# A mixture-of-experts and state-space layer: fixed last tiles, eight early dense groups, and the state's input product taken in the router's pass

## The chip, the cores and the metric

The kernel runs on one core of a Trainium2 chip. The metric is the device time of one execution in microseconds (us). The kernel before took 1827.65 us, the median of three runs (1825.58 to 1830.5). One further execution was profiled; all rows below are from it.

## The reference

The input x has 16 x 512 = 8192 tokens (rows) of 256 features. Everything is float32.

```
xn  = layernorm(x)                          # no weights
out = x + dense(xn) + moe(xn)

dense(x):                                   # a state-space block and a gated feed-forward
  u  = rmsnorm(x) * ssm_w
  Bu = u @ B_w.T                            # 64 states per row
  h_b = sigmoid(log_lambda) * h_(b-1) + Bu_b   # lax.scan over swapaxes(Bu, 0, 1)
  x  = x + h @ C_w.T + D_skip * u
  z  = rmsnorm(x) * ffn_w
  return x + (silu(z @ w1.T) * (z @ w3.T)) @ w2.T      # 688 hidden

moe(h):                                     # 32 experts, 8 chosen per row, inner size 128
  scores  = sigmoid(h @ gate_w.T);  sc = scores + gate_bias
  keep the 4 best of 8 expert groups (by the sum of their two best sc), then the 8 best experts
  weights = 2.5 * scores of the chosen / their sum
  routed  = sum over the chosen of weight * (silu(h @ w_gate.T) * (h @ w_up.T)) @ w_down.T
  shared  = (silu(h @ sh_gate.T) * (h @ sh_up.T)) @ sh_down.T      # 256 hidden
  return routed + shared
```

## The kernel before

The 8192 rows are 64 tiles of 128; four tiles make one of 16 dense groups, and 32 tiles one half of the expert work. Each engine has its instruction stream written out by hand, and semaphores tie them. In order of time:

1. The router's pass (`a0_...`). For each group VectorE and ScalarE normalise x into `rows_of` (half 0 in `big`, half 1 in `xe`), TensorE transposes (`a0_transpose`), ScalarE copies to `a0_xT`, TensorE multiplies with the router's weights (`a0_router`), ScalarE copies the product (L598) and, when it is transposed back, the logits. SP loads x and the constants.
2. SP stores two blocks of zero rows, 9216 KB each, over the last 64 tiles of `sorted_rows` of either half (L398). They pad what no row fills.
3. Nine early dense groups (`FIRST = 9`). The steps s = 0 to 7 of a group are eight hidden tiles: shared expert first (s < 2), then the feed-forward. Woven into them is the preparation of the next group: `transpose_x`, `bu_product` (L1232), VectorE's `bu_scale` (L948), `bu_transpose` (L1239), `scan` (L954), `y_product` (L1245), `make_x1`, `make_z`, `transpose_z`. Also woven in is the routing (`route`, `route_late`): for each half VectorE picks the experts, ranks the rows with TensorE's help, works out the base of each expert's tiles (`r_bases`), and the slot of each row in `sorted_rows` (`r_slot_table`); `r_weights` ends it and signals `routing_done`.
4. GpSimd's scatter. One indirect DMA (L546) per tile and choice writes 128 rows of xn with their weights to their slots, 256 per half. Ahead of it 16 padding stores of GpSimd and 16 of SP (32 of SP for half 1) zero what is left of each expert's last tile.
5. The expert pairs. A half has 288 tiles of 128 sorted rows, worked off in 144 pairs. `one_expert(n)` is true for the first `SAME` = 128 pairs of a half: both tiles belong to one expert, and its gate and up weights are copied once and used for 256 columns. In the other 16 pairs each tile has its own expert, with two weight copies (L1100) and twice the matmuls of half the width (L1348). All expert weights stand in `big`, on top of what the routing and half 0 had there, so their last pieces are loaded when half 0 has been scattered (L420). The results go to DRAM; GpSimd gathers them per row (L557) and VectorE adds them up (`sum_step`), half 0 during the pairs of half 1.
6. Seven late dense groups, the first of which is prepared after the last pair. The adding up of half 1 (`combine`) is woven into them.

Of the kernel before, what the change touches and what calls it, by code (L numbers as in the profile page):

```python
# [5 lines left out]
P = 128  # L6
# [6 lines left out]
ds = bass.ds  # L13
# [6 lines left out]
E = 32  # L20
# [29 lines left out]
def build(nc, x, log_lambda, BT, CT, D_skip, ssm_w, ssm_w_col, ffn_w_col, w13T, w2T, gateT, gate_bias, wexp,  # L50
# [13 lines left out]
    SAME = HT * K // 2  # L64
    USED = 2 * SAME - E
    SPAN = NSLOT + E * P
# [6 lines left out]
    FIRST = 9  # L73
    LATE = range(FIRST, GROUPS)
    QUARTER = HT // 4
# [5 lines left out]
    parts = nc.dram_tensor("parts", [T, D], F32).ap()  # L81
    te_dram = nc.dram_tensor("te_dram", [HALVES, 2, P * TE_C], U32).ap()

    with ExitStack() as ctx:
# [40 lines left out]
        bT = sb("bT", [P, DC, N_STATE])  # L125
        cT = sb("cT", [N_STATE, D])
        gT = sb("gT", [P, DC, E])
# [41 lines left out]
        ne, ntf, endt, base, nt_f, ones_e, full_f, full, unused_f, unused_i = (scratch(E) for _ in range(10))  # L169

        two_f, two, odd, end_odd, apart, cut, first_odd, te_odd, te_late = (logits[:, k * E:(k + 1) * E] for k in range(9))
        two_u = two_f.bitcast(U32)
        first_odd, te_odd, te_late = first_odd[:, 0:1], te_odd[:, 0:TE_C], te_late[:, 0:TE_C]
        nt_u, full_u, unused_u = nt_f.bitcast(U32), full_f.bitcast(U32), unused_i.bitcast(U32)
        in_part = nt_f
# [6 lines left out]
        pad_starts = [scratch(E).bitcast(U32) for _ in range(HALVES)]  # L182
# [12 lines left out]
        ARENA = 9472  # L195
# [9 lines left out]
        bu = take(GT * N_STATE).rearrange("p (t n) -> p t n", n=N_STATE)  # L205
# [12 lines left out]
        a0_lT = [take(G)[0:E, :] for _ in range(2)]  # L218
# [30 lines left out]
        a0_lT_ready = sem("a0_lT_ready")  # L249
# [11 lines left out]
        starts_ready = sem("starts_ready")  # L261
        padded = sems("padded", HALVES)
        padded_by_pool = sem("padded_by_pool")
# [8 lines left out]
        bu_ready = sem("bu_ready")  # L272
        bu_scaled = sem("bu_scaled")
        buT_ready = sem("buT_ready")
# [15 lines left out]
        scattered = [sems(f"scattered{h_}_", 4) for h_ in range(HALVES)]  # L290
# [13 lines left out]
        gathered = sems("gathered", DEEP)  # L304
        part_loaded = sems("part_loaded", RING)
# [5 lines left out]
        CONSTS = 16  # L311
        WEXP_LOADS = 1 + 1 + 4
# [9 lines left out]
        def xn_of(g):  # L322

            if g in LATE:
                return xn_late
            return rows_of[g // 8][:, g % 8 * GT:(g % 8 + 1) * GT, 0:D]
# [32 lines left out]
        def scattered_all(eng, half):  # L359

            for j in range(4):
                eng.wait_ge(scattered[half][j], 16 * K * QUARTER)
# [3 lines left out]
        def _(sp):  # L366
# [9 lines left out]

            for n in range(GROUPS):
                load_x_a0(n)
            for dst, src in ((bT[:, :, :], BT), (ssmw_col[:, :], ssm_w_col),
                             (skip_w[:, :], D_skip.partition_broadcast(P)),  # L380
# [12 lines left out]
            for n in range(GROUPS, GROUPS + 4):  # L393
                load_x_a0(n)

# [5 lines left out]

            def store_padding(half, es):
                sp.wait_ge(starts_ready, half + 1)
                sp.wait_ge(padded[half], 16)
                for e in es:
                    start = sp.value_load(pad_starts[half][0:1, e:e + 1], min_val=0, max_val=SPAN - P)
                    sp.dma_start(sorted_rows[half][ds(start, P), :], pad_row).then_inc(padded[half], 16)
# [18 lines left out]
            store_padding(0, range(E // 2))  # L426
            for g in range(FIRST - 1):
                if g + 4 < FIRST:
# [5 lines left out]
                if g == 3:  # L434
                    store_padding(1, range(E))
                if g == 4:
                    turn_tile_experts(1)
                if g == 5:
                    sp.wait_ge(routing_done, 2)
                    sp.wait_ge(padded[0], 16 * (E // 2 + 1))  # L440
                    sp.wait_ge(padded_by_pool, 16 * (E // 2))
                    sp.wait_ge(padded[1], 16 * (E + 1))
                    load_wexp(0, AT_X)
            sp.wait_ge(x_used, FIRST)
            load_wexp(AT_X, AT_ROWS)
            sp.wait_ge(xposed, FIRST)
            for j in range(4):
                sp.wait_ge(scattered[0][j], 16 * K * QUARTER)
                load_wexp(AT_ROWS + j * QUARTER * ROW, AT_ROWS + (j + 1) * QUARTER * ROW)
            store_part(FIRST - 1)  # L450


# [13 lines left out]
            sp.wait_ge(zposed, FIRST)  # L466
            sp.wait_ge(gu_ready, CH * (FIRST - 1) + 2)
            sp.wait_ge(rms_z_ready, FIRST)
            for n in range(RING):
                load_rows(n)  # L470
            for par in range(2):
                sp.wait_ge(part_stored[par], 16 * len(range(par, FIRST, 2)))
            for m in range(ALL + 2):
                if m < ALL:
# [4 lines left out]
                    if m + RING < ALL:  # L479
                        load_rows(m + RING)  # L480
                n = m - 2
# [11 lines left out]
            sp.wait_ge(wgu_ready, ALL)  # L493
            for g in range(FIRST, FIRST + 4):
                load_x(g, g)
            for i in range(HT, HT + GT):
                load_part(i)
            for g in LATE:
                for t in range(GT):
                    store_out((g - 1) * GT + t)  # L500
                    if t == 2 and g + 4 < GROUPS:
                        sp.wait_ge(x_used, g + 1)
                        load_x(g + 4, g + 4)
# [7 lines left out]
        def _(pool):  # L511
# [16 lines left out]
            nc.gpsimd.iota(unused_u, pattern=[[1, E]], base=NTILE, channel_multiplier=0)  # L528
# [904 lines left out]
```

## Time and profile before

| | |
|---|---|
| median of three runs | 1827.65 us |
| profiled execution | 1828.46 us, span of its records 1826.8 us |
| TensorE | 1732.0 us busy (95%), granted clock 0.969 on average |
| VectorE | 986.1 us (54%) |
| ScalarE | 653.4 us (36%) |
| GpSimd | 1042.6 us (57%) |
| DMA | 383.71 MB, 210 GB/s on average |
| chain that ended last | TensorE 89%, VectorE 7%, others 4% |

The span runs from the first to the last instruction; the time of the execution is 1.66 us longer. The chain is the sequence of work that ended last, followed back from the end. Expert products (L1348) are 29% of it, the dense gate and up products (L1263) 19%. A share of busy time is a mean over stages: which wait ends last has to be read at the borders between them. TensorE's granted clock has two levels, 2.4 GHz (1.00) and 1.2 GHz (0.50).

### The profile page before, as it was taken

What the parts mean: (1) busy time and instruction counts of PE and PEld (TensorE: products, weight loads), DVE (VectorE), ACT (ScalarE), POOL (GpSimd) and SP (SyncE); (2) the same over time, 40 slices, a digit from 0 to 9 for tenths busy, and PEclk for the clock granted to TensorE, in tenths of its full rate; (3) what the DMA queues carried; (4) which work ended last, traced back from release to release, by engine and by line L of the source; (5) the groups of instructions that cost most, each with busy time, mean ns of one, the idle gap of its engine ahead of it and who ended that gap; (6) DMA issues with size and microseconds to landing.
All of it is one profiled execution on the core that took longest, in us unless ns stands there. A gap on an engine that the chain in (4) does not pass through costs nothing.

```text
span 1826.8 us, 26818 instructions
## 1 busy us (share of the span) xinstructions
PE 1732.0 (95%) x7846; PEld 1259.9 (69%) x7848; DVE 986.1 (54%) x2832; ACT 653.4 (36%) x1349; POOL 1042.6 (57%) x1058
## 2 busy tenths in 40 slices
PE   7797899899998999999999999999999969999996
PEld 3464565566666888888889888888888846666663
DVE  7487646633313444444445566666666535555555
ACT  6520221222213444444444444444444422222220
POOL 0002777777777777773000566666656077777773
PEclk9798999899998999999999999999999969999998
DMA  5964333636378999997555899999899554443332
GB/s 171 323 224 139 134 140 115 223 128 252 126 277 274 297 292 300 293 296 248 180 176 179 255 295 274 287 276 288 275 284 277 175 158 123 123 121 110 110 110 75
DMA packets 270790, 383.71 MB, mean 210 GB/s; under 512 B 30916, under 2 KB 235832, under 8 KB 269880
## 3 DMA queue, kind: packets, MB, share of 16 engines
q1 hardware_dynamic: 220584, 236.94, 41.1%
q0 software_dynamic: 49920, 145.03, 24.1%
q8 instruction: 66, 1.08, 0.2%
q14 instruction: 76, 0.62, 0.1%
q10 hardware_dynamic: 144, 0.03, 0.0%
HBM read 189.47 MB, written 192.42 MB: 209 GB/s over the span
## 4 chain that ended last, share of the span: by engine, by line
PE 89%; DVE 7%; issue 1%; ACT 1%; DMA 1%; DVEq 0%; SPq 0%; ACTq 0%
PE ps L1348 29%; PE ps L1263 19%; PE ps L1362 14%; PE ps L1280 11%; PE ps L1336 7%; PE ps L1183 2%; PE ps L1245 2%; PE ps L1216 2%; PE ps L1255 1%; PE ps L1232 1%; PE ps L1176 1%; DVE big L1009 1%; DMA big<-in_x 0%; PE ps L1239 0%; DVE arena L991 0%
## 5 line engine op out<-in xcount | busy, mean ns | idle before, releaser
L557 POOL DMA_INDIRECT xe<-results,slots x384 | 391.9, 1020 | 395.8 <-DMA results<-arena 217.4
L1348 PE MATMUL ps<-arena 128*128 128x256 f32 (+1 forms) x2560 | 573.5, 369 | 1.5 <-ACT arena L675 1.5
L1348 PEld LDWEIGHTS ps<-arena 128*128 128x128 f32 x2560 | 428.6, 190 | 106.1 <-ACT arena L675 66.0
L1100 DVE COPY arena<-big 128x512 f32 x320 | 138.7, 442 | 345.4 <-PE ps L1348 318.6
L546 POOL DMA_INDIRECT sorted_rows<-big,slots x256 | 260.5, 1017 | 84.0 <-issue 77.8
L1362 PE MATMUL ps<-big,arena 128*128 x1152 | 296.4, 380 | 0.3 <-DVE arena L1108 0.3
L546 POOL DMA_INDIRECT sorted_rows<-xe,slots x256 | 248.3, 970 | 78.1 <-issue 78.1
L1263 PE MATMUL ps<-arena,w 128*128 128x512 f32 x640 | 288.4, 593 | 0.0
L648 ACT ACTIVATE arena<-ps 128x512 f32<-128x512 f32 (+1 forms) x128 | 76.4, 597 | 559.4 <-PE ps L1263 515.5
L991 DVE TENSOR_TENSOR arena<-arena,ps 128x512 f32<-128x512 f32 (+1 forms) x128 | 88.0, 688 | 329.3 <-ACT arena L648 328.2
L680 ACT ACTIVATE arena<-ps 128x256 f32<-128x256 f32 x288 | 110.6, 384 | 377.0 <-PE ps L1348 377.0
L1362 PEld LDWEIGHTS ps<-big,arena 128*128 128x128 f32 x1152 | 196.4, 190 | 15.4 <-issue 0.7
L1263 PEld LDWEIGHTS ps<-arena,w 128*128 128x128 f32 x640 | 122.2, 191 | 119.5 <-issue 115.2
L1280 PE MATMUL ps<-w,arena 128*128 128x256 f32 (+1 forms) x768 | 186.3, 385 | 1.7 <-DVE arena L991 1.7
L675 ACT ACTIVATE arena<-ps 128x512 f32<-128x512 f32 x288 | 172.1, 597 | 26.1 <-PE ps L1336 11.0
L1336 PE MATMUL ps<-ident,arena 128*128 128x128 f32 x1152 | 173.8, 274 | 6.4 <-DMA arena<-sorted_rows 6.4
L1280 PEld LDWEIGHTS ps<-w,arena 128*128 128x128 f32 (+1 forms) x768 | 142.8, 191 | 50.7 <-issue 31.1
L1117 DVE TENSOR_SCALAR arena<-ps,wcol 128x256 f32<-128x256 f32 x288 | 139.0, 483 | 68.1 <-PE ps L1362 60.4
L690 ACT ACTIVATE arena<-ps,wcol 128x256 f32<-128x256 f32 x288 | 136.6, 474 | 92.6 <-PE ps L1362 91.0
L1336 PEld LDWEIGHTS ps<-ident,arena 128*128 128x128 f32 x1152 | 143.5, 141 | 32.8 <-issue 6.9
L557 POOL DMA_INDIRECT big<-results,slots x128 | 130.4, 1019 | 39.0 <-issue 39.0
L1263 PE MATMUL ps<-arena,shgu 128*128 128x512 f32 x256 | 123.4, 638 | 7.1 <-DVEq L819 7.1
(186 smaller groups left out, 1402.8 us busy)
## 6 DMA issues: line engine op xcount, KB each, us to landing
arena<-sorted_rows SPq DMA_DIRECT2D x288, 288.0 KB
results<-arena SPq DMA_DIRECT2D x288, 256.0 KB, 3.6
sorted_rows<-big SPq DMA_DIRECT2D x2, 9216.0 KB, 47.3
big<-in_x SPq DMA_DIRECT2D x32, 512.0 KB, 4.5
sorted_rows<-big SPq DMA_DIRECT2D x48, 144.0 KB, 1.9
xe<-results,slots POOLq DMA_INDIRECT x384, 4.0
out<-xe SPq DMA_DIRECT2D x48, 128.0 KB, 3.9
big<-in_wexp SPq DMA_DIRECT2D x1, 5632.0 KB, 19.3
```

Of the source, the lines that this page charges most:

```text
L546: pool.indirect_dma_start(out=sorted_rows[half], out_offset=bass.IndirectOffsetOnAxis(ap=slots[:, half * HT + t, k:k + 1], axis=0), in_=ro ...
L557: pool.indirect_dma_start(out=gathered_at[place(i)][:, k, :], out_offset=None, in_=results[half], in_offset=bass.IndirectOffsetOnAxis(ap=s ...
L675: nc.scalar.activation(rT[n % 2], ps[:, n % 2, :], ACT.Copy).then_inc(rT_ready, 1)
L680: nc.scalar.activation(eg[n % 2], ps[:, 2 + n % 2, 0:2 * P].rearrange("p (s i) -> p s i", s=2), ACT.Silu).then_inc(eg_ready, 1)
L690: nc.scalar.activation(ey[n % RING][:, 0, :], ps[:, 4 + 2 * (n % 2), 0:D], ACT.Copy, scale=wcol[:, n % RING, 0:1]).then_inc(ey_act, 1)
L1100: last = nc.vector.tensor_copy(wgu[n % 2][:, s, :], big[:, ds(at_w, 4 * INNER)])
L1117: tsc(ey[n % RING][:, 1, :], ps[:, 5 + 2 * (n % 2), 0:D], wcol[:, n % RING, 1:2], None, ALU.mult).then_inc(ey_dve, 1)
L1263: last = mm(ps[:, 2 + 2 * (s % 2) + u, :], w[:, u, c, lo:lo + P], src[:, c, :], start=c == 0, stop=c == DC - 1)
L1280: last = mm(ps[:, 6 + t // 2, (t % 2) * D:(t % 2 + 1) * D], h[c % HR][at_p, t * P:(t + 1) * P], w, start=False, stop=s == CH - 1 and t % 2 ...
L1336: last = tp(ps[:, n % 2, j * P:(j + 1) * P], rows[n % RING][:, s, c * P:(c + 1) * P], ident[:, :])
L1348: last = mm(ps[:, 2 + n % 2, (2 * u + s) * P:(2 * u + end) * P], wgu[n % 2][:, s, at_w:at_w + INNER], rT[n % 2][:, (2 * c + s) * P:(2 * c ...
L1362: last = mm(ps[:, 4 + 2 * (n % 2) + s, 0:D], eh[n % 2][:, s, :], big[:, ds(at_w + 2 * D, D)], start=True, stop=True)
```

## The change

- **Fixed last tiles.** Each expert's last, partly filled tile now has a fixed place: tile 256 + e for expert e, inside the region that is zeroed at the start. The padding stores that depended on the counts go (16 on GpSimd, 48 on SP). Only full tiles are paired, so a half has 96 pairs of one expert and 48 of two. The slot table has a second correction, and the tile-to-expert table four more small steps.
- **Eight early groups.** `FIRST` is 8. Group 8 is prepared inside group 7, and its `xT`, `zT` and part are stored to DRAM and read back behind the expert pairs; its eight steps are the first of the late stage.
- **The input product in the router's pass.** `first_w` holds the state's and the router's weights side by side, one product gives 64 + 32 rows. ScalarE copies them and issues a store of the 64 rows to `bu_dram`. The reciprocal norms are turned to rows (`turn_rinv`, `copy_rinv`) and stored too. SP reads both back for each group (`load_bu`); VectorE multiplies and scans. `bu_product`, `bu_scale` and `bu_transpose` are gone, the scan stands at s = 2 rather than 3, the y product at s = 3 rather than 4.
- The scatter signals in eighths of a half rather than quarters.

```diff
-    SAME = HT * K // 2
-    USED = 2 * SAME - E
-    SPAN = NSLOT + E * P
+    FULL_TILES = HT * K
+    SAME = FULL_TILES // 2 - E
+    USED = FULL_TILES - E
+    SPAN = NSLOT
-    FIRST = 9
+    FIRST = HT // GT
...
@@ SP @@
+            def load_bu(n):
+                sp.wait_ge(bu_stored[n % 2], 16 * (n // 2 + 1))
+                sp.wait_ge(rinv_stored, 16 * (n // 8 + 1))
+                if n:
+                    sp.wait_ge(y_ready, n)
+                sp.dma_start(bu, bu_dram[n]).then_inc(bu_loaded, 16)
+                sp.dma_start(hs, rinv_dram[n * GT:(n + 1) * GT, :].rearrange("t p -> (t p)").partition_broadcast(N_STATE)
+                             ).then_inc(bu_loaded, 16)
...
             for n in range(GROUPS, GROUPS + 4):
                 load_x_a0(n)
+            load_bu(0)
...
-            store_padding(0, range(E // 2))
+            load_bu(1)
             for g in range(FIRST - 1):
...
                 store_part(g)
+                load_bu(g + 2)
...
@@ GpSimd @@
-            pool.wait_ge(starts_ready, 1)
-            pool.wait_ge(padded[0], 16)
-            for e in range(E // 2, E):
-                start = pool.value_load(pad_starts[0][0:1, e:e + 1], min_val=0, max_val=SPAN - P)
-                pool.dma_start(sorted_rows[0][ds(start, P), :], pad_row).then_inc(padded_by_pool, 16)
...
@@ ScalarE @@
                 act.wait_ge(a0_products_ready, g + 1)
-                nc.scalar.activation(a0_lT[g % 2], ps[0:E, 4 + g % 2, :], ACT.Copy).then_inc(a0_lT_ready, 1)
+                if g >= 2:
+                    act.wait_ge(bu_stored[g % 2], 16 * (g // 2))
+                nc.scalar.activation(a0_first[g % 2], ps[0:N_STATE + E, 4 + g % 2, :], ACT.Copy
+                                     ).then_inc(a0_first_ready, 1)
+                act.wait_ge(a0_first_ready, g + 1)
+                act.dma_start(bu_dram[g], a0_first[g % 2][0:N_STATE, :]).then_inc(bu_stored[g % 2], 16)
...
@@ VectorE @@
             def scan(n):
-                dve.wait_ge(buT_ready, n + 1)
-                nc.vector.tensor_tensor_scan(hs, lam_b[:, :], ps[0:N_STATE, 1, :], 0.0, ALU.mult, ALU.add
-                                             ).then_inc(hs_ready, 1)
+                dve.wait_ge(bu_loaded, 32 * (n + 1))
+                do(tt(bu, bu, hs, ALU.mult))
+                nc.vector.tensor_tensor_scan(hs, lam_b[:, :], bu, 0.0, ALU.mult, ALU.add).then_inc(hs_ready, 1)
...
                     if more and s == 2:
-                        bu_scale(g + 1)
-                    if more and s == 3:
                         scan(g + 1)
...
-            dve.wait_ge(ey_act, ALL)
-            a1_norm(FIRST)
-            bu_scale(FIRST)
-            scan(FIRST)
-            make_x1(FIRST)
-            make_z(FIRST)
...
@@ TensorE @@
-                    if more and s == 2:
-                        bu_product(g + 1)
-                    if more and s == 3:
-                        bu_transpose(g + 1)
-                    if more and s == 4:
+                    if more and s == 3:
+                        pe.wait_ge(xT_ready, g + 2)
                         y_product(g + 1)
...
-            transpose_x(FIRST)
-            bu_product(FIRST)
-            bu_transpose(FIRST)
-            y_product(FIRST)
-            transpose_z(FIRST)
+            pe.wait_ge(xT_reloaded, 16)
```

ScalarE in the router's pass, before; L598 is the copy of the product, L602 that of the logits:

```order
L572 ACTIVATE rstd<-mv,ln_eps 128x4 [waits var_ready]
L598 ACTIVATE arena<-ps 32x512 [waits a0_products_ready]
L602 ACTIVATE big<-ps 128x128 [waits a0_logits_ready]
L580 ACTIVATE big<-big,nmr,rstd 128x256 [waits nmr_ready]
L580 ACTIVATE big<-big,nmr,rstd 128x256
```

The same place now:

```order
L602 ACTIVATE rstd<-mv,ln_eps 128x4 [waits var_ready]
L630 ACTIVATE arena<-ps 96x512 [waits bu_stored0,a0_products_ready]
L633 DMA bu_dram<-arena 64x512 [waits a0_first_ready]
L651 ACTIVATE big<-ps 128x128 [waits a0_logits_ready]
L610 ACTIVATE big<-big,nmr,rstd 128x256 [waits nmr_ready]
L610 ACTIVATE big<-big,nmr,rstd 128x256
```

Between the two copies stands the issue of a store, behind a wait for the copy ahead of it.

SP's queue at the end of the router's pass, before; the two rows of 128x64x288 are the zero blocks:

```order
L392 DMA shd<-in_shdT 128x512
L369 DMA big<-in_x 128x4x256 [waits a0_xn_act,a0_xn_dve] x4
L398 DMA sorted_rows<-big 128x64x288 [waits routing_consts_made]
L398 DMA sorted_rows<-big 128x64x288
L406 TENSOR_LOAD big [waits padded0,starts_ready]
```

And now, with the input product and the factors of groups 0 and 1 (`bu_dram`, `rinv_dram`):

```order
L416 DMA shd<-in_shdT 128x512
L385 DMA big<-in_x 128x4x256 [waits a0_xn_act,a0_xn_dve] x4
L398 DMA arena<-bu_dram 64x512 [waits rinv_stored,bu_stored0]
L399 DMA arena<-rinv_dram 64x512
L423 DMA sorted_rows<-big 128x64x288 [waits routing_consts_made]
L423 DMA sorted_rows<-big 128x64x288
L398 DMA arena<-bu_dram 64x512 [waits y_ready,rinv_stored,bu_stored1]
L399 DMA arena<-rinv_dram 64x512
L385 DMA big<-in_x 128x4x256 [waits x_used]
```

Group 0's loads stand ahead of the zero blocks, group 1's behind them.

SP's queue where the experts begin, now; before, the row loads (`arena<-sorted_rows`) waited for the dense groups alone, and the last piece of expert weights stood ahead of them:

```order
L438 DMA big<-in_wexp 128x4096 [waits x_used]
L486 DMA parts<-arena 128x4x256
L461 DMA arena<-sorted_rows 128x2x288 [waits scattered0_3,scattered0_2,scattered0_4,scattered0_1,scattered0_5,scattered0_0,scattered0_6,z_ready,scattered0_7,y_ready,xT_stored]
L461 DMA arena<-sorted_rows 128x2x288 x3
L438 DMA big<-in_wexp 128x1152 [waits scattered0_7]
L495 DMA kept_zT<-arena 128x1024 [waits zT_ready]
L442 DMA parts<-arena 128x4x256 [waits part_ready]
```

Rows, the last weights, the kept `zT` and group 7's part now follow the last scatter.

## Rows read from the trace of the kernel before

**Rows 1.** Chain of waits: start us, us, what; starts of three groups.
```profile
461.65 7.06 PE ps L1263 x16
508.13 7.06 PE ps L1263 x16
...
1770.21 7.06 PE ps L1263 x16
```

**Rows 2.** Timeline, SP and TensorE, before the experts: start us, us, instruction, idle before.
```profile
549.92 0.38 SPq L424 DMA_DIRECT2D parts<-arena  x1
...
556.72 3.78 PE L1348 MATMUL ps<-arena 128*128 128x256 f32 x8 [0.77 <-ACT arena L675]
```

**Rows 3.** The scatter's line: duration ns min/median/max, first and last start.
```profile
L546 POOL DMA_INDIRECT sorted_rows<-big,slots x256: 957/963/4916, 181.2 to 518.5; - x128
L546 POOL DMA_INDIRECT sorted_rows<-xe,slots x256: 959/963/1187, 519.7 to 844.8; - x128
...
DMA to landing us min/median/max: 2.4/2.5/16.5
```

**Rows 4.** Timeline of VectorE in groups 0 and 1.
```profile
110.39 0.42 DVE L948 TENSOR_TENSOR arena<-ps,rinv 128x256 f32<-128x256 f32 x1
...
113.50 1.20 DVE L954 TENSOR_TENSOR_SCAN arena<-lam_b,ps 64x512 f32<-64x512 f32 x1
117.33 0.69 DVE L991 TENSOR_TENSOR arena<-arena,ps 128x512 f32<-128x512 f32 x1 [2.63 <-ACT arena L648]
...
153.26 1.22 DVE L857 TENSOR_TENSOR big<-big 128x1024 f32<-128x1024 f32 x1
...
166.86 1.23 DVE L875 TENSOR_TENSOR big<-big 128x1024 f32<-128x1024 f32 x1
```

**Rows 5.** The zero blocks' line: issue ns min/median/max, starts, landing.
```profile
L398 SPq DMA_DIRECT2D sorted_rows<-big x2: 1458/13469/25480, 61.6 to 63.1; - x2
...
DMA to landing us min/median/max: 33.7/47.3/60.9
```

**Rows 6.** Timeline of ScalarE in the router's pass, one group of 16.
```profile
50.98 0.59 ACT L598 ACTIVATE arena<-ps 32x512 f32<-32x512 f32 x1 [0.35 <-PE ps L1183]
51.47 0.25 ACT L602 ACTIVATE big<-ps 128x128 f32<-128x128 f32 x1
```

**Rows 7.** Timeline: the issues of two small loads.
```profile
0.94 0.43 ACTq L566 DMA_DIRECT2D gT<-in_gateT  x1
...
49.95 1.09 SPq L392 DMA_DIRECT2D cT<-in_CT  x1
```

**Rows 8.** Timeline of TensorE, prologue and group 0; the last row from the chain.
```profile
75.47 3.78 PE L1245 MATMUL ps<-cT,arena 64*128 64x256 f32 x8 [1.37 <-DVE arena L954]
...
102.82 1.90 PE L1232 MATMUL ps<-bT,arena 128*128 128x64 f32 x16
104.55 1.95 PE L1280 MATMUL ps<-shd,arena 128*128 128x256 f32 x8
...
116.59 1.99 PE L1245 MATMUL ps<-cT,arena 64*128 64x256 f32 x8
...
176.17 0.44 PE ps L1239 x4
```

**Rows 9.** Chain at pair 128 of half 1; and busy times of the stretch behind it.
```profile
1404.97 1.82 PE ps L1348 x8
...
1408.09 1.87 PE ps L1348 x16
...
1408.09:1458.90 50.81, 50.55 (x382) 45.98 (x382) 31.94 (x103) 23.05 (x48) 6.49 (x7) 1.00 0.62 190
```

**Rows 10.** Timeline behind the pairs: last output, first product of group 9.
```profile
1459.95 0.48 DVE L1117 TENSOR_SCALAR arena<-ps,wcol 128x256 f32<-128x256 f32 x1 [0.91 <-PE ps L1362]
...
1489.32 9.10 PE L1263 MATMUL ps<-arena,shgu 128*128 128x512 f32 x16
```

**Rows 11.** Timeline of GpSimd: its last gather.
```profile
1801.96 0.95 POOL L557 DMA_INDIRECT big<-results,slots  x1 [0.30 <-issue]
```

More of the change, by code:

```diff
@@ L217, in build @@
         a0_xT = [take(DC * G).rearrange("p (c n) -> p c n", c=DC) for _ in range(2)]
-        a0_lT = [take(G)[0:E, :] for _ in range(2)]
+        a0_first = [take(G)[0:N_STATE + E, :] for _ in range(2)]
+        rinvT = take(P)[0:HT, :]
         at[0] = 0
@@ L288, in build @@
         part_stored = sems("part_stored", 2)
[L290 removed]
+        scattered = [sems(f"scattered{h_}_", PIECES) for h_ in range(HALVES)]
         wexp_loaded = sem("wexp_loaded")
@@ L359, in scattered_all @@
         def scattered_all(eng, half):
-            for j in range(4):
-                eng.wait_ge(scattered[half][j], 16 * K * QUARTER)
+            for j in range(PIECES):
+                eng.wait_ge(scattered[half][j], 16 * K * PIECE)
         @block.sync
@@ L756, in _ @@
                     a0_stats(g + 4)
+                if g == -3:
+                    dve.wait_ge(router_loaded, 16 * FIRSTS)
+                    for c in range(DC):
+                        last = tsc(first_w[:, c, 0:N_STATE], first_w[:, c, 0:N_STATE], ssmw_col[:, c:c + 1], None,
+                                   ALU.mult)
+                    last.then_inc(bT_folded, 1)
+                if g == 5:
+                    rms_x(0)
+                if g == 6:
+                    invert_rms_x(0)
+            rms_x(1)
+            invert_rms_x(1)
             def r_pairs(half):
@@ L849, in r_bases @@
                 tsc(base, base, float(P), 1.0, ALU.mult, ALU.add)
-                tsc(apart, apart, float(P), None, ALU.mult)
-                do(tt(full, full, unused_f, ALU.add))
-                tsc(pad_starts[half], full, float(P), None, ALU.mult).then_inc(starts_ready, 1)
+                tsc(apart_part, apart_part, float(P), None, ALU.mult)
+                do(tsc(apart, apart, float(P), None, ALU.mult))
             def r_slot_table(half):
-                by_expert, past = (a.rearrange("p (e t) -> p e t", t=HT) for a in (work, wt))
@@ L857, in r_slot_table @@
-                do(tt(past, by_expert, cut.unsqueeze(2).to_broadcast([P, E, HT]), ALU.is_ge))
-                do(tt(past, past, apart.unsqueeze(2).to_broadcast([P, E, HT]), ALU.mult))
+                by_expert, past, past_full = (a.rearrange("p (e t) -> p e t", t=HT) for a in (work, wt, table))
+                tt(past, by_expert, cut.unsqueeze(2).to_broadcast([P, E, HT]), ALU.is_ge)
+                do(tt(past_full, by_expert, cut_part.unsqueeze(2).to_broadcast([P, E, HT]), ALU.is_ge))
+                tt(past, past, apart.unsqueeze(2).to_broadcast([P, E, HT]), ALU.mult)
@@ L859, in r_slot_table @@
+                do(tt(past_full, past_full, apart_part.unsqueeze(2).to_broadcast([P, E, HT]), ALU.mult))
+                do(tt(wt, wt, table, ALU.add))
                 do(tt(work, work, wt, ALU.add))
```

286 lines of the change are left out of this document (162 added, 124 removed).

## The prediction

> **What bounds the kernel now.** I read the chain of waits first, then the stage borders on it. TensorE carries the chain in three stages: nine early dense groups, 288 expert pairs, seven late dense groups. Dense groups follow each other 46.5 us apart (461.65 to 508.13, [rows 1]). The ninth ends where its part is stored, at 549.92, and the first expert product starts at 556.72 [rows 2]. GpSimd's scatter of half 0 was over by then: 256 indirect DMAs from 181.2 to 519.7, 338.5 us or 1.32 us each, landing 2.5 us after issue [rows 3]. So today the experts wait for the ninth group, and the scatter has about 30 us to spare. VectorE's routing for half 0 comes before the scatter; it ends at 166.86 + 1.23 = 168.1 [rows 4].
>
> The change removes the ninth group from the early stage, so the scatter becomes the candidate for the bound. Everything ahead of it (router pass, padding, routing) then counts in full, which it did not before.
>
> **Router pass.** ScalarE gets a store of the input product for every group, behind a wait for its own copy. The copy takes 0.59 us and its successor starts after 0.49 [rows 6]; the wait adds 0.10, its semaphore some 0.05 (estimate), and the issue 0.43 by ScalarE's only issue before [rows 7]. Of these 0.58 us the idle 0.35 ahead of the same copy [rows 6] hides a part. I take 0.27 for what is left, 13 times until the loads of x are done: 3.5 us. The bounds are 0 and, with SP's dearest small issue of 1.09 us for 64 partitions [rows 7], (0.15 + 1.09 - 0.35) x 13 = 11.6 us. Turning the reciprocals to rows twice makes ScalarE wait for TensorE and VectorE; I put 2 us (bounds 0 and 4). The router's product grows from 32 to 96 output rows with the same 512 columns, hidden. SP issues two more loads ahead of the padding, 0.9. The padding starts 6.4 us later.
>
> **The wait that is added.** The two padding stores are issued at 61.6 and 63.1, and land 33.7 and 60.9 us later, at 95.3 and 124.0 [rows 5]. The second lands 28.7 us after the first though it was issued 1.5 us behind it: SP's queue works them off one after the other. The load of the input product for group 1 now stands on that queue behind both. With the 6.4 us the padding is through at 130.4 and the load, 256 KB with its factors, at about 132.2. VectorE waits for it at step s=2 of group 0, in order, with the top-8 steps, h tiles and the whole routing chain behind it; by its steps before (the input product's scaling at 110.39, [rows 4]) it would be there near 115. Multiplication and scan (1.2 us, [rows 4]) end at T = 134.1. Without the change the scan ended at 113.50 + 1.20 = 114.7.
>
> From the scan to the end of routing took 168.1 - 114.7 = 53.4 us. Now the y product comes before gate/up product 4. TensorE will have stood still for over 15 us, and after such a stop rows show the lower clock: the y product took 3.78 us in the prologue and 1.99 in group 0 [rows 8]. So until h tile 4: y 3.8, the down product 3.1 (partly slow), gate/up 3.5 (half of 7.06, [rows 1]), gate and semaphores 0.9, together 11.3 (7.9 at the full clock), where it had been 117.33 - 114.7 = 2.6 [rows 4]. That adds 8.7. The slot table gets three more operations of 1.22 us [rows 4] and the base computation loses about 1.5 us of small ones: +2.2. Routing ends at T + 64.3 = 198.4.
>
> The Trainium skill, "DMA: Bandwidth & Descriptors", section "Queues, rings and completion order", says that each DMA engine consumes one queue's descriptors in ring order but takes turns between the queues of SP and ACT. By that rule the load on SP's queue must wait while ScalarE's stores need not; the trace agrees for SP's queue [rows 5], and no run here shows the turns.
>
> **Scatter and the experts' start.** The small padding stores, 16 by GpSimd and 16 + 32 by SP, go; the scatter starts 0.3 us after the routing rather than 13 us after it. At 1.32 us each, less 3 us for the vanished stores, 256 take 335 us (bounds 324 at the steady 1.27 of the second half's 325.1 us [rows 3], and 345). 198.7 + 335 = 533.7, landed 536.2. Then SP issues four row loads, the last expert piece, the kept z and the last part, 2.8 MB. Before it was 1.7 MB in 556.72 - 549.92 = 6.8 us [rows 2]; the extra 1.1 MB at some 330 GB/s (9.4 MB per 28.7 us, [rows 5]) and two issues more give 11.2. First expert product at 547.4, 9.3 us earlier.
>
> Would the dense groups end later? Each loses the input product, 104.55 - 102.82 = 1.73, and its transposes, 0.44, 2.2 us together [rows 8]. From the end of routing to the ninth group's start it was 508.13 - 168.1 = 340.0 [rows 1, 4]; now it is 340.0 - 6 x 2.2 + 2.2 (the second slot table) = 329.0, so the eighth ends at 527.4, and with some 8 us of seam experts could start at 535.6. No: the scatter is last, and the early groups' saving pays nothing.
>
> **Experts.** Pairs with one expert fall from 256 to 192, those with two rise from 32 to 96. A one-expert pair takes 1408.09 - 1404.97 = 3.12 us, one with two 3.18, as its product part is 1.87 against 1.82 [rows 9]; 64 x 0.056 = +3.6 us. The second weight copy on VectorE is hidden: in the stretch of two-expert pairs with sums it was busy 31.94 of 50.81 us. Last pair's output ends at 1459.95 + 0.48 = 1460.4 [rows 10], 903.7 after the first; now X = 547.4 + 903.7 + 3.6 = 1454.7.
>
> **Late stage.** Before, the prologue of group 9 stood open: 1460.4 to 1489.32, 28.9 us [rows 10]. Now xT is reloaded inside the pairs, zT needed only at s=2, and group 8 starts 0.6 us after X. The load and normalisation of x for group 9 come just late: 1.5 us. So 0.6 + 45.8 + 6 x 44.3, and from the last group's start to the end 1826.8 - 1770.21 = 56.6 as before [rows 1]: 368.9 us, where it was 366.4. GpSimd's last gather began at 1801.96 [rows 11], 342 after the pairs' end; it has one group more, so it stays hidden.
>
> **Sum.** 1454.7 + 368.9 = 1823.6 against the span 1826.8, -3.2. The profiled execution took 1828.46, 1.7 more than its span; so 1825.2, and 1824.4 against the median of 1827.65. In short: -9.3 at the first border, +3.6 in the pairs, +2.5 after them.
>
> **Rivals.**
> *No queueing.* If the load of group 1 passes the padding, VectorE scans at once, T is 116.6, the clock stays up, routing ends 60.9 later at 177.5, the scatter has landed at 515.3, first product at 526.5: 1804. Against it: the 28.7 us between the two landings. For it: only that the load is small.
> *Quicker scatter.* At 324 us the scatter lands at 525 and the dense end (535.6) decides: 1813. For it the second half's 325 us; against, that half ran beside less VectorE work.
> *ScalarE held by SP's issue.* The second padding issue kept SP 25.5 us [rows 5]. If ScalarE's last stores cannot be issued meanwhile, it stands until about 95, group 0 starts near 115 instead of 93, reaches its scan at 137, T = 139.2, with TensorE at its full clock: routing ends at 139.2 + 60.9 = 200.1, 1826. The Trainium skill, "Perfetto Trace Analysis", section "DMA Instruction — HWDGE (DVE, Sync)", says that the block that writes descriptors is shared between sequencers, which would be this mechanism; no row here shows it.
> *Slower.* ScalarE's 16 stores. Each us they add to the router pass moves padding, scan, routing, scatter and experts alike, since nothing later has slack. At 1.09 us per issue the pass grows by 11.6 rather than 3.5, and with the turning at its bound of 4 that is 1834.5. From 0.72 us per issue on the change gains nothing. For it the SP row of 1.09; against it ScalarE's own 0.43.
>
> **How the numbers follow.** What can be told from no change is about 0.3%, 5.5 us: faster is below 1822.2, slower above 1833.1. The forecast has 0.47, own range 1815 to 1833 (faster 0.13, same 0.27, slower 0.07). No queueing 0.15 (faster), quicker scatter 0.12 (faster), ScalarE held 0.10 (same 0.07, slower 0.03), slower stores 0.16 (slower 0.14, same 0.02). Sum: faster 0.40, same 0.36, slower 0.24. The range 1806 to 1838 leaves out most of the first rival and the far end of the last.
>
> **What would show it.** VectorE idle at its multiply in group 0 until the padding has landed, near 132; L546's counterpart starting near 199; TensorE idle some 15 to 20 us between the eighth group and the first expert product, released by rows or the last piece of expert weights; late groups 44.3 us apart; no gap of 29 us behind the pairs. The prediction is wrong if the scan of group 1 ends before 120, if the scatter ends before TensorE's early groups, if the router pass lengthens by more than 10 us, or if a two-expert pair takes over 3.25 us.

## The result and the profile after

The changed kernel took 1840.08 us, the median of five runs (1835.92 to 1840.98), beside 1827.81 for the kernel before on the same chip: a ratio of 1.0059, 95% interval 1.0047 to 1.0071. It is slower by 12.3 us. The forecast was 1824.4, in a range of 1806 to 1838. The profiled execution has a span of 1838.3 us, 14.7 more than the 1823.6 of the prediction's sum.

**The wait on SP's queue.** The timeline of SP after the router's pass:

```profile
67.25 0.59 SPq L399 DMA_DIRECT2D arena<-rinv_dram  x1
67.89 27.24 SPq L423 DMA_DIRECT2D sorted_rows<-big  x2
95.24 29.63 SPq L398 DMA_DIRECT2D arena<-bu_dram  x1
124.91 1.40 SPq L399 DMA_DIRECT2D arena<-rinv_dram  x1
```

L423 is the padding (L398 in [rows 5]), L398 and L399 are the two loads of the input product and its factors. Behind the padding not only the transfer waits: the issue of a 128 KB load stands on SP for 29.63 us. The padding's own line, and ScalarE's stores of the input product, first the issue in ns with the first and last start, then the landing:

```profile
L423 SPq DMA_DIRECT2D sorted_rows<-big x2: 578/13598/26617, 67.9 to 68.5; - x2
...
DMA to landing us min/median/max: 33.7/48.4/63.1
```

```profile
L633 ACTq DMA_DIRECT2D bu_dram<-arena x16: 452/453/516, 19.5 to 71.7; - x16
...
DMA to landing us min/median/max: 2.3/3.3/6.4
```

Padding started 6.3 us later than in [rows 5], at 67.9; the forecast was 68.0. ScalarE's 16 stores took 0.45 us each. Two were issued after 68.3, while SP stood in the second padding issue, and neither they nor ScalarE were held. VectorE and TensorE at the scan of group 1 (in square brackets the idle time before the instruction and what ended it):

```profile
133.18 0.68 DVE L1025 TENSOR_TENSOR arena<-arena 64x512 f32<-64x512 f32 x1 [17.07 <-DMA arena<-rinv_dram]
133.89 1.22 DVE L1026 TENSOR_TENSOR_SCAN arena<-lam_b,arena 64x512 f32<-64x512 f32 x1
```

```profile
135.25 3.75 PE L1305 MATMUL ps<-cT,arena 64*128 64x256 f32 x8 [21.48 <-DVE arena L1026]
138.93 3.78 PE L1340 MATMUL ps<-w,arena 128*128 128x256 f32 x8
142.51 4.58 PE L1323 MATMUL ps<-arena,w 128*128 128x512 f32 x8
```

From 135.2 to 147.1 TensorE's granted clock was 0.61 on average, the lower level for the first two of these rows. At the full clock the same three took 1.99 us [rows 8], 1.89 (from 146.92) and 3.60 (from 148.65): the clock cost 4.6 us behind the stop.

**Routing and scatter.** Routing of half 0 ended at 199.59 + 1.23 = 200.8, where it was 168.1 [rows 4]. The scatter, half 0 and half 1, to be set beside [rows 3]:

```profile
L574 POOL DMA_INDIRECT sorted_rows<-big,slots x256: 956/960/4566, 201.8 to 544.0; - x128
```

```profile
L574 POOL DMA_INDIRECT sorted_rows<-xe,slots x256: 956/960/1212, 545.3 to 870.5; - x128
```

Half 0 takes 342.2 us from first to last start, 337.3 before; half 1 takes 325.2 and 325.1.

**The border to the experts.** TensorE's eighth group starts at 499.96 and is followed by VectorE's last add to its part; then SP, TensorE, ScalarE and VectorE:

```profile
499.96 1.55 PE L1323 MATMUL ps<-arena,shgu 128*128 128x512 f32 x3
...
550.28 1.09 PE L1394 MATMUL ps<-ident,arena 128*128 128x128 f32 x4 [6.00 <-DMA arena<-sorted_rows]
562.73 2.90 PE L1406 MATMUL ps<-arena 128*128 128x256 f32 x6 [11.36 <-DVE arena L1166]
```

```profile
546.81 1.98 SPq L461 DMA_DIRECT2D arena<-sorted_rows  x4
548.84 0.47 SPq L438 DMA_DIRECT2D big<-in_wexp  x1
549.35 0.43 SPq L495 DMA_DIRECT2D kept_zT<-arena  x1
549.83 0.44 SPq L442 DMA_DIRECT2D parts<-arena  x1
```

```profile
561.10 0.60 ACT L732 ACTIVATE arena<-ps 128x512 f32<-128x512 f32 x1 [17.62 <-DMA parts<-arena]
```

```profile
544.32 1.28 DVE L1069 TENSOR_TENSOR arena<-arena,ps 128x512 f32<-128x512 f32 x2 [3.21 <-PE ps L1340]
562.16 0.77 DVE L1166 COPY arena<-big 128x512 f32 x2 [16.55 <-issue]
```

The scatter is last at 546.8, but the dense groups end at 545.6, level with it. Then SP's 2.8 MB are moved until 561, and the first product (L1406, L1348 before) starts at 562.73, 6.0 us later than in [rows 2]. TensorE's waits in groups 1 and 3, for VectorE:

```profile
201.78 1.65 PE L1340 MATMUL ps<-shd,arena 128*128 128x256 f32 x3 [11.37 <-DVE arena L1062]
...
317.29 0.88 PE L1305 MATMUL ps<-cT,arena 64*128 64x256 f32 x3 [3.94 <-DVE arena L1026]
```

The first is 7.06 us in the kernel before (at 169.05), and the second, a wait for the scan, is not there. Group 4 has one like the first, 10.80 us for 6.56.

**Pairs and late groups.** The expert line, first and last start, and the first gate and up products behind the pairs and in the last group:

```profile
L1406 PE MATMUL ps<-arena x3072: 275/371/766, 562.7 to 1467.0; 128*128 128x256 f32 x96, 128*128 128x128 f32 x96
L1420 PE MATMUL ps<-big,arena x1152: 379/379/478, 570.3 to 1469.1; 128*128 x192
```

```profile
1470.35 1.96 PE L1323 MATMUL ps<-arena,shgu 128*128 128x512 f32 x4 [0.83 <-DVE arena L1185]
...
1781.60 4.99 PE L1323 MATMUL ps<-arena,shgu 128*128 128x512 f32 x11
```

The gap of 29 us behind the pairs [rows 10] is gone, and behind the first of them late groups follow each other 44.3 us apart (1516.09 to 1781.60 in six steps) instead of 46.5.

### The profile page after: what moved, and what is told of

Same layout as the page of the kernel before. It is cut to its first block, busy times and chain, and to the rows that moved or that the text cites. A ratio compares the mean times of both kernels' runs of the same rounds, so it can differ in the third digit from the quotient of the medians.

```text
span 1838.3 us, 27059 instructions
## 1 busy us (share of the span) xinstructions
PE 1702.5 (93%) x8040; PEld 1250.5 (68%) x8042; DVE 1010.7 (55%) x2899; ACT 654.9 (36%) x1352; POOL 1042.3 (57%) x1042
## 4 chain that ended last, share of the span: by engine, by line
PE 69%; POOL 14%; issue 5%; DVE 4%; SPq 3%; DMA 2%; ACT 2%; ACTq 0%; DVEq 0%; POOLq 0%
PE ps L1406 29%; POOL sorted_rows L574 14%; PE ps L1420 14%; PE ps L1323 10%; PE ps L1394 7%; PE ps L1340 6%; SPq L398 2%; SPq L423 1%; PE ps L1305 1%; PE ps L1315 1%; PE ps L1290 1%; DMA bu_dram<-arena 1%; DMA parts<-arena 1%; DMA big<-in_x 1%; ACT arena L622 1%
## 5 line engine op out<-in xcount | busy, mean ns | idle before, releaser
L1406 PE MATMUL ps<-arena 128*128 128x256 f32 (+1 forms) x3072 | 577.1, 336 | 12.0 <-DVE arena L1166 11.4
L1406 PEld LDWEIGHTS ps<-arena 128*128 128x128 f32 x3072 | 455.7, 191 | 106.7 <-ACT arena L732 76.6
L574 POOL DMA_INDIRECT sorted_rows<-big,slots x256 | 265.5, 1037 | 276.3 <-DVEq L947 198.6
L1166 DVE COPY arena<-big 128x512 f32 x384 | 160.0, 438 | 356.1 <-PE ps L1406 322.1
L702 ACT ACTIVATE arena<-ps 128x512 f32<-128x512 f32 (+1 forms) x128 | 76.3, 596 | 565.8 <-PE ps L1323 524.4
L1340 PE MATMUL ps<-w,arena 128*128 128x256 f32 (+1 forms) x768 | 191.7, 394 | 3.4 <-DVE arena L1062 3.4
L1340 PEld LDWEIGHTS ps<-w,arena 128*128 128x128 f32 (+1 forms) x768 | 147.1, 195 | 61.0 <-issue 37.6
## 6 DMA issues: line engine op xcount, KB each, us to landing
big<-in_wexp SPq DMA_DIRECT2D x1, 5632.0 KB, 18.7
```

Source lines behind the costliest of these rows:

```text
L574: pool.indirect_dma_start(out=sorted_rows[half], out_offset=bass.IndirectOffsetOnAxis(ap=slots[:, half * HT + t, k:k + 1], axis=0), in_=ro ...
L1166: last = nc.vector.tensor_copy(wgu[n % 2][:, s, :], big[:, ds(at_w, 4 * INNER)])
L1340: last = mm(ps[:, 6 + t // 2, (t % 2) * D:(t % 2 + 1) * D], h[c % HR][at_p, t * P:(t + 1) * P], w, start=False, stop=s == CH - 1 and t % 2 ...
L1406: last = mm(ps[:, 2 + n % 2, (2 * u + s) * P:(2 * u + end) * P], wgu[n % 2][:, s, at_w:at_w + INNER], rT[n % 2][:, (2 * c + s) * P:(2 * c ...
```

## The experiments

Eleven kernels. Ratios are to the kernel before, with 95% intervals; runs 7 and 8 were executed once.

| run | edit | us | ratio |
|---|---|---|---|
| changed kernel | | 1840.1 | 1.0059 (1.0047 to 1.0071) |
| 1 | padding behind the load of group 1 | 1821.1 | 0.9965 (0.9952 to 0.9979) |
| 2 | only half 1's padding behind it | 1821.0 | 0.9969 (0.9957 to 0.9981) |
| 3 | padding left, load issued by ScalarE | 1822.2 | 0.9976 (0.9966 to 0.9987) |
| 4 | looser waits at the border | 1836.9 | 1.0058 (1.0044 to 1.0071) |
| 5 | kernel before + fixed tiles alone | 1840.7 | 1.0074 (1.0060 to 1.0088) |
| 6 | 1 + 4 + order of the border's transfers | 1815.9 | 0.9933 (0.9920 to 0.9947) |
| 7, 8 | 6 + repeated adds | 1820.6, 1827.0 | |
| 9 | 6 + scan from PSUM | 1818.2 | 0.9952 (0.9939 to 0.9966) |
| 10 | 6 without the fixed tiles | 1815.5 | 0.9937 (0.9924 to 0.9951) |
| 11 | 10 + scan from PSUM | 1818.0 | 0.9949 (0.9935 to 0.9963) |

### Run 1: the padding behind the load

```
-            for half in range(HALVES):
-                sp.dma_start(sorted_rows[half][USED * P:NSLOT, :] ...).then_inc(padded[half], 16)
...
             load_bu(1)
+            for half in range(HALVES):
+                store_padding(half)          # the same store
```

> Both padding stores are issued by SP behind the load of the input product for group 1 instead of ahead of it. Theory (queue order is the loss): the load lands before VectorE needs it at 116.1, the idle of 17.07 us before its multiply and TensorE's 21.5 us go, routing ends near 181 instead of 200.8, scatter 181.5 to 525, dense end near 524, first expert product near 543: 20 us less than 1840.1, about 1820. Rival (the DMA engines are simply full, the order does not matter): the load still lands near 133 and the time stays at 1840. Second rival (scatter and dense end do not follow the routing one to one, for the padding now runs beside group 0): under half of the 20 us comes back, about 1832.

Measured 1821.05, 19.0 less. SP's timeline, and the scatter's line:

```profile
84.20 0.45 SPq L398 DMA_DIRECT2D arena<-bu_dram  x1
84.70 0.59 SPq L399 DMA_DIRECT2D arena<-rinv_dram  x1
85.33 24.88 SPq L423 DMA_DIRECT2D sorted_rows<-big  x2
110.25 29.06 SPq L385 DMA_DIRECT2D big<-in_x  x1
```

```profile
L576 POOL DMA_INDIRECT sorted_rows<-big,slots x256: 956/960/4573, 183.1 to 525.0; - x128
```

The wait of 29 us has not gone; it now stands before a load of x that nobody wants before group 3. Scan ends at 116.9 (135.1), scatter starts at 183.1 (201.8), the first weight copy at 542.2 (562.2): 18.3, 18.7, 20.0 us. What the scan loses, the end loses. By the ratios the gain is 17 us rather than 19. TensorE stood for 4.4 us instead of 21.5, and its clock was at the lower level behind it all the same:

```profile
117.00 3.75 PE L1307 MATMUL ps<-cT,arena 64*128 64x256 f32 x8 [4.41 <-DVE arena L1028]
```

### Run 2: one store ahead, one behind

```
+            store_padding(0)
             load_bu(1)
+            store_padding(1)
```

> Only the padding store of half 1 is issued behind the load of the input product for group 1; that of half 0 stays ahead of it. Theory (the load waits exactly for what stands ahead of it on SP's queue): half 0's store is through at 101.6, the load lands at 104 to 110, still before VectorE's 116.1, so the whole stall goes as with both moved: about 1820. If the stall grows with the time of the store rather than ending at its landing, or if the store of half 1 takes engine time from the load, half of it stays (idle of 5 to 10 us before the multiply): about 1830.

1820.97, and no wait before the multiply. SP:

```profile
67.80 0.58 SPq L423 DMA_DIRECT2D sorted_rows<-big  x1
84.17 10.76 SPq L398 DMA_DIRECT2D arena<-bu_dram  x1
94.97 1.37 SPq L399 DMA_DIRECT2D arena<-rinv_dram  x1
```

The load's issue stands for 10.8 us, until 94.9, behind one store of 9.4 MB, and for 29.6 behind two. One store ahead fits into the time until VectorE wants the load at 116; two do not.

### Run 3: the load on ScalarE's queue

```
-            load_bu(1)                       # SP
...
+            act.wait_ge(y_ready, 1)
+            act.dma_start(bu, bu_dram[1]).then_inc(bu_loaded, 16)
+            act.dma_start(hs, rinv_dram[GT:2 * GT, :] ...).then_inc(bu_loaded, 16)
             zT_copy(0)
```

> The padding stays where it is; the load of the input product for group 1 and its factors is issued by ScalarE, ahead of its zT copy of group 0. Theory (the queue, not the DMA engines, holds the load): issued near 85 to 93, landed 3 to 10 us later in the middle of the padding, no stall at VectorE, two issues of 0.5 us each ahead of group 0: about 1821. Rival (16 DMA engines busy with 9.4 MB per half hold any load): landed only after 131, time 1840 or more, since ScalarE's issue may stand as well.

1822.24. ScalarE's timeline and what the view of DMAs says of its queue (KB each, us from issue to landing), in the middle of the padding:

```profile
89.81 0.47 ACTq L724 DMA_DIRECT2D arena<-bu_dram  x1
90.31 1.35 ACTq L725 DMA_DIRECT2D arena<-rinv_dram  x1
```

```profile
arena<-bu_dram ACTq DMA_DIRECT2D x1, 128.0 KB, 5.7
arena<-rinv_dram ACTq DMA_DIRECT2D x1, 128.0 KB, 6.7
```

So the DMA engines were not closed to the load; the queue was. Both loads landed by 97.0, with the padding in flight until about 133. The Trainium skill, "DMA: Bandwidth & Descriptors", section "Queues, rings and completion order", says that a DMA engine takes turns between the queues of SP and ACT; this run agrees. The Trainium skill, "Perfetto Trace Analysis", section "DMA Instruction — HWDGE (DVE, Sync)", says that the block that writes descriptors is shared between sequencers; no holding of ScalarE's issues is seen here, 0.47 and 1.35 us while SP stood in the padding's two issues for 27.5.

### Run 4: looser waits at the border

```
# ScalarE: both part_stored waits dropped; SP: dropped
# VectorE:
-            for par in range(2):
-                dve.wait_ge(part_stored[par], 16 * len(range(par, FIRST, 2)))
+            dve.wait_ge(part_stored[0], 16 * len(range(0, FIRST, 2)))
+            dve.wait_ge(part_kept, 16)
```

> Behind the eighth dense group VectorE waits for the stored parts of even groups and the kept part only (the others are not overwritten by expert tiles), ScalarE's first copy of turned rows for none, SP for none. Padding as in the changed kernel. Theory (the last part's store, fourth in the queue, costs the seam about 5 us): first weight copy near 557 instead of 562.16, bounded by the last piece of expert weights, issued at 548.84; 5 us less, about 1835. Rival (all the transfers of the seam share one bandwidth and land together, 2.8 MB): within 1 us of 1840.

```profile
557.54 0.78 DVE L1162 COPY arena<-big 128x512 f32 x2 [14.06 <-issue]
```

The first weight copy came at 557.5, as expected. The median fell by 3.2 us, but the ratio is that of the changed kernel (1.0058 and 1.0059), so a gain in the whole time is not shown by this run. Between the scatter's landing and this copy there are now 10.6 us, most of them for the last piece of expert weights, issued at 549.0.

### Run 5: the fixed tiles alone

The edit is the diff of the tiles put on the kernel before: `SAME` 96, `USED`, `r_bases`, `r_slot_table`, `r_tile_experts`, and no small padding stores; nine early groups, no store or load of the input product.

> The kernel before with the fixed zeroed last tiles alone: nine early dense groups, the input product per group, no store or load of it. By the theory (the early dense groups end last in this form, so a scatter that starts sooner gains nothing, and the pairs cost 64 x 0.056 us more): scatter starts near 171 instead of 181.2 and ends near 512, the ninth group's part is stored near 550 as before, pairs +3.6, and 2 us of slot table on VectorE's way: 1831 to 1833 against 1827.7. Rival (the tiles carry a gain of their own, since 48 small stores and their waits are gone): 1824 or less.

1840.74: 12.9 us more, not 4, and the profiled execution shows 9.9 of them. TensorE at the ninth group and the first pair, and the expert and scatter lines:

```profile
513.77 1.55 PE L1243 MATMUL ps<-arena,shgu 128*128 128x512 f32 x3
```

```profile
561.88 1.65 PE L1328 MATMUL ps<-arena 128*128 128x256 f32 x3 [0.77 <-ACT arena L655]
```

```profile
L1342 PE MATMUL ps<-big,arena x1152: 379/379/478, 571.4 to 1470.2; 128*128 x192
```

```profile
L526 POOL DMA_INDIRECT sorted_rows<-big,slots x256: 956/960/4962, 171.0 to 507.7; - x128
```

The ninth group starts 5.6 us later than in [rows 1]: 3 us from the slot table of half 0, 3 from that of half 1, on VectorE, for which TensorE waits in groups 1 and 4. From first product to last down product the pairs take 908.3 instead of 902.8, +5.5. The scatter, 10 us earlier and without the small stores, takes 336.7 between its starts instead of 337.3: taking the stores away made it no shorter. Both expectations fell; this part alone costs as much as the whole change.

### Run 6: padding and border together

```
+            sp.dma_start(kept_zT, zT...).then_inc(zT_stored, 16)
+            store_part(FIRST - 1)
             scattered_all(sp, 0)
-            for n in range(RING):
-                load_rows(n)
+            load_rows(0)
             load_wexp_over_rows(PIECES - 1)
+            for n in range(1, RING):
+                load_rows(n)
```

> Both repairs: the padding is issued behind the load for group 1, and at the seam the kept z and the last part are stored before the wait for the scatter, then row load 0, the last piece of expert weights, row loads 1 to 3, with the looser waits of the fourth kernel. Theory (seam bounded by what is issued between the scatter's landing and the first weight copy): scatter landed near 527.5, row load and piece issued in 1 us and 0.87 MB landed 4 us later, first weight copy near 533 instead of 542.2: 9 us less than 1821.0, 1812. Rival (dense groups end level with the scatter, so stores move behind the last group and nothing but the 4.7 us of the loosened wait is won): 1816.

```profile
524.84 0.33 SPq L493 DMA_DIRECT2D kept_zT<-arena  x1
526.96 0.37 SPq L442 DMA_DIRECT2D parts<-arena  x1
529.32 0.37 SPq L463 DMA_DIRECT2D arena<-sorted_rows  x1
529.74 0.49 SPq L438 DMA_DIRECT2D big<-in_wexp  x1
```

```profile
536.25 0.76 DVE L1165 COPY arena<-big 128x512 f32 x2 [9.38 <-issue]
```

1815.91, the fastest with run 10, and 0.67% below the kernel before. The copy came 6.0 us earlier than in run 1, 9 had been expected: the scatter's last landing slipped from 527.5 to 529.3 beside the two stores that were moved ahead of it, and the piece of weights took 5.2 us rather than 4. Of the 15 us between scatter and first copy, 7 are left.

### Runs 7 and 8: does VectorE hold the scatter?

```
# 7, groups 2 to 7, three times ahead of the add itself:
+                        do(tt(part_of(n), x_of(n), x1, ALU.add))       # both inputs from SBUF
# 8, likewise:
+                        ... tt(x1[...], z[...], ps[:, b, :] ..., ALU.add)  # one from PSUM
```

> As the kernel with padding and seam, and for the groups 2 to 7 VectorE's add of x and x1 (both read from SBUF, 1.22 us) is done four times instead of once, to the same place: 18 more operations, 22 us of VectorE. Theory (GpSimd's indirect DMA is held while VectorE runs an operation that reads both inputs from SBUF): the 256 scatters, 265.1 us of busy time at a floor of 0.96 each, grow by 0.7 to 3.5 us per group, 4 to 21 in all. Rival (the long scatters are chance, or of the DMA engines): busy time within 2 us of 265.

> The same with the two adds into x1 (one input from SBUF, one from PSUM, 1.28 us the pair) done four times: as much more time of VectorE as in the run with repeated adds of x and x1. Theory: only two inputs from SBUF hold GpSimd, so the 256 scatters stay within 2 us of 265. Rival (any work of VectorE slows GpSimd): they grow as in that run. In both runs the early groups may end later, by up to 3.8 us a group.

The scatter's group, of run 7 and of run 8 (busy us, mean ns, idle):

```profile
L575 POOL DMA_INDIRECT sorted_rows<-big,slots x256 | 263.8, 1030 | 258.4 <-DVEq L946 180.7 <-issue 77.7
```

```profile
L575 POOL DMA_INDIRECT sorted_rows<-big,slots x256 | 265.8, 1038 | 259.2 <-DVEq L946 181.5 <-issue 77.7
```

The theory fell: 18 more operations with two inputs from SBUF left the scatter at 263.8 us, 265.2 without them. Beside the three added ones from 426.16 to 429.91 the four indirect DMAs took 0.96, 1.01, 0.96 and 0.96 us. The runs showed something else. The scatter ended as before (last starts 524.4 and 527.3), but the dense groups ended 4.2 and 12.1 us later than in run 6, and the first weight copy 5.5 and 13.6 us later. So the dense groups stand level with the scatter, and by these rows a shorter scatter alone would have given next to nothing.

### Runs 9 to 11: the scan's input, and the old tiles

```
# 9
-                do(tt(bu, bu, hs, ALU.mult))
-                nc.vector.tensor_tensor_scan(hs, lam_b[:, :], bu, ...)
+                dve.wait_ge(xT_ready, n + 1)
+                do(tt(ps[0:N_STATE, 1, :], bu, hs, ALU.mult))
+                nc.vector.tensor_tensor_scan(hs, lam_b[:, :], ps[0:N_STATE, 1, :], ...)
```

Run 10 is run 6 with the tiles, small padding stores and `SAME` of the kernel before; run 11 is both edits.

> On top of padding and seam: VectorE writes the scaled input product into PSUM and the scan reads it from there, as in the kernel before; so only one of the scan's inputs comes from SBUF. In the runs so far 3.0 to 5.8 us of the scatters' time above their floor lay beside this scan, and nothing in the kernel before. Theory (a scan with both inputs in SBUF holds GpSimd's indirect DMA): the 256 scatters fall from 265.2 to 261 to 262 us, none is long beside the scan, and the time falls by 1 to 2 us only, for the dense groups end level: 1814 to 1815. Rival (as the repeated adds suggested, the place of an operation makes no difference): busy time within 1 us of 265.2.

> Padding and seam repaired, and the fixed zeroed last tiles undone: small padding stores again, 16 by GpSimd and 48 by SP, 256 one-expert pairs and 32 with two. Theory (the tiles cost 5.5 us in the pairs and some 3 us of slot table per half, and give back only the 13 us between routing and scatter, which now count since the scatter is last): scatter from 190 to 528 instead of 183.3 to 526, first weight copy +2.5, pairs -5.3: 1813 against 1815.9. Rival A (undoing them gains what they cost alone, 12.9 us): 1803. Rival B (the fixed tiles pay here, since the scatter starts 13 us later without them): 1820 or more.

> The old tiles and the scan from PSUM together, on top of padding and seam. With the old tiles the dense groups end some 6 us before the scatter, so the scatter's 3 to 4 us count in full here, if the scan is what lengthens it: 3 us less than the run with old tiles alone. If the place of the scan makes no difference: the same within 1 us.

Run 9, run 10, run 11:

```profile
L575 POOL DMA_INDIRECT sorted_rows<-big,slots x256 | 261.4, 1021 | 259.3 <-DVEq L946 181.5 <-issue 77.7
```

```profile
L595 POOL DMA_INDIRECT sorted_rows<-big,slots x256 | 261.4, 1021 | 83.5 <-issue 77.7 <-DMA sorted_rows<-big 5.8
```

```profile
L595 POOL DMA_INDIRECT sorted_rows<-big,slots x256 | 262.3, 1025 | 83.4 <-issue 77.7 <-DMA sorted_rows<-big 5.7
```

In run 9 the scatter's busy time fell by the 3.8 us that were expected and the time did not: the intervals of runs 6 and 9 overlap. The execution of run 9 that was profiled was the fastest of its five, 1813.3 us beside 1818.0 to 1819.0, so its rows do not tell what made the others longer; in it the scatter landed 2.6 us earlier than in run 6 and the first weight copy came 0.9 us earlier. With the old tiles the same edit took nothing off (262.3 against 261.4). So the scatter's 4 us depend on more than the place of the scan, and their cause stays open. Run 10 gave 1815.5, level with run 6; 1813 was expected, and neither rival came. The pairs are 5.6 us shorter (902.5 against 908.1); the first product is 5.8 us later (542.6), for the scatter starts at 193.6 instead of 183.3 and ends 6.5 later. And the first mechanism showed up again: the 16 small stores stand ahead of the next load, and VectorE waits:

```profile
194.17 0.68 DVE L1044 TENSOR_TENSOR arena<-arena 64x512 f32<-64x512 f32 x1 [8.48 <-DMA arena<-rinv_dram]
```

## Why the prediction was wrong

The mechanisms were the right ones, and so was their order. What failed are two terms of the sum and the start that they were counted from: the scatter, 335 us forecast and 343.5 measured, and the border behind it, 11.2 and 15.9 us, after a start 3.1 us late. All lay on the one path without slack, so the first expert product came 6.0 us later than before, not 9.3 us earlier. None of the four signs that were to show the prediction wrong came: the scan ended at 135, the scatter (545.0) no earlier than TensorE's eighth group (544.3), the pass grew by 6.3 us, a two-expert pair took 3.18.

- *Router pass and added wait: right.* Padding at 67.9 (68.0 forecast), end of the scan 135.1 (134.1). In part this is luck: SP's two loads ahead of the padding took 2.4 us and not 0.9, and ScalarE's share was as much smaller. Runs 1 to 3 show that the queue is the cause, and that it costs 18 to 19 us: without it the change is a gain of 0.35%. The rival of ScalarE being held is refuted.
- *Scan to end of routing: right in the main, 65.7 us for 64.3.* The lower clock was there and cost 4.6 us, where 3.4 had been put. But it does not hang on the padding. In run 1, where TensorE stood 4.4 us, the same three products took 3.75, 3.78 and 4.17 us, and scan to scatter 66.2 us for 66.7. What the padding's place costs is the length of the stop; the lower clock behind the scan stays when it is moved. In the kernel before TensorE did not wait for this scan, and the y product took 1.99 us. No run put the y product back to its old step, so that the new step is what brings the stop of 4.4 us is argued and not shown.
- *The scatter: "less 3 us for the vanished stores" was wrong.* Run 5 shows that they cost it 0.6. With a later start by 3.1 us (201.8, not 198.7) and 7.5 more until it had landed, this is the largest part of the error, though 343.5 us lay inside the bound of 345. Some 5 us of it are longer single DMAs, not longer gaps: the 256 were busy 265.5 us, 260.5 before and 259.9 in run 5. Runs 9 and 10 took 4 us of this away, each in its own way, run 11 with both edits did not; the cause stays open.
- *Border: 11.2 forecast, 15.9 measured.* 1.7 MB had been priced at the 6.8 us of the border before, and 1.1 MB more at the 330 GB/s of the padding. But in those 6.8 us the engines moved 270 GB/s, 1.8 MB with half 1's scatter in it: the old border never held all of the 1.7 MB. From 546.8 to 561.1 they now moved 4.6 MB at 320 GB/s, 2.8 of SP and some 1.8 of the scatter, and ScalarE and VectorE waited for the last transfer in the queue, not for the ones they use (runs 4 and 6).
- *"The scatter is last": right by 1.2 us only.* The eighth group was forecast to end at 527.4; TensorE was through at 544.3 and the part ready at 545.6. What each group saves was subtracted six times, but only from group 5 on do the rows show it (44.2 us a group for 46.5). Groups 1 to 4 took 70.7, 48.8, 56.1 and 60.8 us, where they had taken 65.3, 48.3, 51.8 and 58.5: TensorE waits longer there for VectorE, which has more to do now, and for the scan. Runs 7 and 8 show the dense end at the border.
- *Pairs and late stage: right.* 907.4 us (907.3) and 368.2 (368.9). Other runs with the new tiles gave 908.1 to 908.3 for first product to last down product, where this one gave 906.4, so +5.5 rather than +3.6 is the tiles' price.

In sum 3.1 + 7.5 + 4.7 + 0.1 - 0.7 = 14.7 us. The rival *no queueing*, 1804, had the same terms too small: run 1, where the wait is gone, took 1821. The rival on the slower side, ScalarE's stores, was not what happened (0.45 us each); the slower result came from several terms of a few us on a path where I had said myself that nothing later has slack.

Of the three parts of the change, the tiles cost 12.9 us alone (run 5), and nothing with the padding moved and the border loosened (runs 6 and 10), where the pairs' 5.6 us and the scatter's earlier start make up for each other. Eight early groups and the input product in the router's pass gave 19.7 us on top (run 1 against run 5), and the place of the padding took 19.0 of them back (medians).

## What to carry over

Before a small load is put on a queue, read what stands ahead of it there: a store that nobody waits for costs its whole duration when a load that somebody waits for is behind it. Moving it behind, or the load to another queue, gave 18 to 19 us here. Where two long streams end within a microsecond of each other, price both to their end, and count on a gain in one only up to the other's.

## What the runs showed of the hardware

- The sequencer itself stands: SP's issue of a 128 KB load took 29.6 us behind two stores of 9.4 MB, 10.8 us behind one, 0.45 with the queue free. ScalarE's issues while SP stood took 0.31 to 1.35 us (changed kernel and run 3).
- An indirect DMA of GpSimd takes 0.96 us and 0.30 between two, but single ones took up to 4.6, beside VectorE's work on SBUF: the longest, 4.57 us from 309.91, ended 0.4 us after VectorE's L881, one operation of 4.67 us from 309.46 with both inputs in SBUF. The Trainium skill, "SBUF — State Buffer", section "SBUF: two separate sides", says that a VectorE operation with two inputs in SBUF holds off a GpSimd operation that reads SBUF. This row and run 9 (-3.8 us) agree; run 7, with 18 more such operations and no change, does not, nor does run 11.
- TensorE's clock was at the lower level behind a stop of 4.4 us as behind one of 21.5: the y product took 3.75 us both times, 1.99 at the full clock.
